# A graph network's edge stage on one core: SyncE fetches the set-aside rows one round earlier

## The chip, the cores and the metric

One core of a Trainium2 chip runs the whole program. The metric is device time in microseconds (us), the median of several executions. The engines are TensorE (PE, matmuls; PEld its weight loads), VectorE (DVE), ScalarE (ACT), GpSimd (POOL) and SyncE (SP, which here only issues transfers). A name with a q (SPq, ACTq) is that engine's instruction queue, where DMA issues stand.

## The reference, cut to what matters

Two graph layers over 6,250 nodes and 200,000 edges, sorted by destination. The stage that the change touches is the second layer, per edge:

```python
w = jax.nn.silu(rbf @ We1 + be1) @ We2 + be2      # edge_attr (200000 x 64) -> 128 per edge
m = w * (h[src] @ Wlin)                           # row of lin_table, picked by src
agg = jax.ops.segment_sum(m, dst, num_segments=h.shape[0])
out = jax.nn.silu(agg @ Wn1 + bn1) @ Wn2 + bn2
return h + out
```

## The kernel before

`h @ Wlin` stands in device memory as `lin_table` (one 512-byte row per node) when the edge stage begins. The edges are cut into G = 196 groups of 1,024 (8 tiles of 128 edges), and four groups make a round; there are ITERS = 49 rounds. Buffers are a ring of RING = 4 slots, so a round fills each slot once.

For every group, in this order:

- SP loads 1,024 rows of edge_attr into the slot of `ea` (`load_ea`, L505; one 256 KB transfer). It may do so when the group four back has been transposed (`ea_turned`).
- PE transposes them (`turn_ea`, L1678), ACT copies the result (`features`, L849), PE multiplies by We1 (`layer1`, L1686), ACT applies silu (`silus`, L856), PE multiplies by We2 (`layer2`, L1693 and L1697) into the PSUM tensor pb.
- POOL gathers the source rows tile by tile into the slot of `gat` (`gather`, L596, indirect DMA of 128 rows), by an index column that ACT copies (`next_idx`, L727) after its other work for a group.
- DVE multiplies pb by the rows (`messages`, L1336) and counts `msg_ready`, two per group. POOL may refill the slot after that.
- DVE compares destinations (L1340), PE sums by destination (`group_sums`, L1714), DVE adds the sums (L1353).

PE runs the groups as a software pipeline: for group g it does layer2(g), layer1(g+1), turn_ea(g+2), group_sums(g-1).

The eighth tile of the fourth group of a round is set aside: for rounds 1 to PICKS = 47 POOL does not gather it. Its 128 rows are fetched one by one with plain 512-byte transfers into `aside[par]` (two buffers, by the round's parity): 72 by SP and 56 by ACT, in four chunks of 18 and 14. `fetch_rows` does a chunk: a register load of the list (L418), then the transfers (L422). In the messages of that fourth group DVE waits for `sp_rows_in[par]` and `act_rows_in[par]`, then multiplies three quarters at L1330 and the last quarter with the aside rows at L1332. ACT fetches the rows of round it+1 while it handles round it (`source_rows`, with a wait on `msg_ready` at L860 before the first chunk). SP's `load_turn(it)` loads the four edge groups of round it, and after each of them fetches a chunk of round it-1.

Of the kernel before, what the change touches and what calls it, by code (L numbers as in the profile page):

```python
# [32 lines left out]
RING = 4  # L33
# [22 lines left out]
PICKS = ITERS - 2  # L56
SP_ROWS = 72
# [12 lines left out]
def gnn_kernel(nc, x, src, dst, edge_attr, W1, b1, W2, b2, We1, be1, We2, be2, Wlin, Wn1, bn1, Wn2, bn2, out):  # L70
    ctx = ExitStack()
    with ctx:
# [3 lines left out]
        def sem(name):  # L76
            return ctx.enter_context(nc.semaphore(name))
# [54 lines left out]
        def part(mem, at, n, dt=fp32):  # L132

            v = mem[:, at:at + n]
            return v if dt is fp32 else v.bitcast(dt)
# [77 lines left out]
        sp_list = part(table_w, 2 * F, PICKS * SP_ROWS, int32)[0:1, :].rearrange("a (k r) -> a k r", r=SP_ROWS)  # L213
# [154 lines left out]
        sp_rows_in = [sem(f"sp_rows_in{i}") for i in range(2)]  # L368
# [10 lines left out]
        msg_ready = sem("msg_ready")  # L379


        passed = sem("passed")
# [57 lines left out]
        def _(sp):  # L440
# [76 lines left out]
            def load_turn(it, par=None):  # L517
                for s in range(RING):
                    sp.wait_ge(ea_turned, it * RING + (s - RING + 1))
                    load_ea(it * RING + s, s)  # L520
                    if par is not None:
                        fetch_rows(sp, sp_list, it - 1, par, s, 0, SP_ROWS // RING, sp_rows_in)
            load_turn(1)
            with sp.Fori(0, PICKS // 2) as i:
                load_turn(i * 2 + 2, 1)
                load_turn(i * 2 + 3, 0)
            for s in range(RING):
                g = (ITERS - 1) * RING + s
                sp.wait_ge(ea_turned, g - RING + 1)
                fetch_rows(sp, sp_list, PICKS, 1, s, 0, SP_ROWS // RING, sp_rows_in)  # L530
                if g < G - 1:
                    load_ea(g, s)
                else:

                    rest = g * GE + FULL_TAIL * P
                    sp.dma_start(ea[:, s, 0:FULL_TAIL * RBF].rearrange("p (u f) -> p u f", u=FULL_TAIL),
                                 edge_attr[g * GE:rest, :].rearrange("(u p) f -> p u f", u=FULL_TAIL)).then_inc(ea_loaded[s], 16)
                    sp.dma_start(ea[0:N_EDGES - rest, s, FULL_TAIL * RBF:(FULL_TAIL + 1) * RBF],
                                 edge_attr[rest:N_EDGES, :]).then_inc(ea_loaded[s], 16)
# [1254 lines left out]
```

## Time and profile before

| | us |
|---|---|
| median of 3 executions (4439.01 to 4446.9) | 4445.35 |
| the profiled execution | 4483.88 |
| its span, first to last instruction | 4482.2 |
| stretch 0 to 1444: first layer, node work | 1444 |
| stretch 1444 to 1525: the edge stage begins, no row fetched by SP yet | 81 |
| stretch 1525 to 4423: SP fetches rows of rounds 1 to 47 | 2898 |
| stretch 4423 to 4482: last groups, output | 59 |
| TensorE's granted clock in the third stretch, share of full speed | 0.70 |
| busy in the third stretch: PE, POOL, DVE, ACT | 1594, 1393, 766, 387 |

Busy time counts an engine's own work; issuing transfers, register work and waiting are not busy. No engine is busy for even 60% of the third stretch, so what sets its length has to be looked for in the queues and waits.

### The profile page before, as it was taken

To read this page: it belongs to the slowest core of one execution; us is meant where nothing else is said; L and a number is where in the kernel's file an instruction comes from. 1 tells how busy PE (TensorE), PEld (TensorE's weight loads), DVE (VectorE), ACT (ScalarE), POOL (GpSimd) and SP (SyncE) were. 2 spreads that over 40 slices of the span, in tenths; PEclk is the share of its full clock that TensorE was granted. 3 is DMA by queue.
4 is the path that set the end of the run, shared out by engine and by line. 5 is a ranking of instruction groups with operands and counts; after the bars stand their busy time and mean duration, and the time that the engine had idled before them with its cause. 6 is when DMAs were issued, how large, how long until landed. Compare 5 with 4: busy or idle time off the path is not lost.

```text
span 4482.2 us, 78117 instructions
## 1 busy us (share of the span) xinstructions
PE 2954.2 (66%) x18158; PEld 2128.8 (47%) x18159; DVE 1957.4 (44%) x4445; ACT 963.7 (22%) x2058; POOL 1504.8 (34%) x1605
## 2 busy tenths in 40 slices
PE   4789999999799554565555555545655555555547
PEld 2335667676599333443333443334433334433335
DVE  4999998888744322222222222222222222222223
ACT  3213345555311211111111111111111111111111
POOL 5000000000000544544454544444444445444442
PEclk6999999999899676766666766666777676777668
DMA  2001122222397211211121212111211121111212
GB/s 63 1 30 58 73 87 100 104 102 102 158 354 284 59 53 51 53 51 50 49 54 51 55 49 53 51 52 52 53 48 51 52 53 53 50 52 51 53 50 57
DMA packets 291040, 327.33 MB, mean 73 GB/s; under 512 B 237087, under 2 KB 250424, under 8 KB 278174
## 3 DMA queue, kind: packets, MB, share of 16 engines
q1 hardware_dynamic: 234382, 218.90, 14.7%
q0 software_dynamic: 51072, 104.27, 8.1%
q14 instruction: 302, 2.47, 0.2%
q10 hardware_dynamic: 5264, 1.36, 0.1%
q8 instruction: 20, 0.33, 0.0%
HBM read 239.30 MB, written 85.09 MB: 72 GB/s over the span
## 4 chain that ended last, share of the span: by engine, by line
SPq 42%; issue 29%; PE 13%; DVE 10%; DVEq 4%; another core or an unknown queue 2%; DMA 0%; ACT 0%; POOL 0%; ACTq 0%; POOLq 0%
SPq L422 28%; SPq L418 10%; DVE shared L1131 3%; SPq L505 3%; PE pc L1522 3%; PE pd L1522 3%; PE pb L1528 2%; PE pa L1528 2%; DVE c L1131 1%; DVE c L1136 1%; DVEq L1131 1%; DVE hch L1131 1%; DVE loop L1131 1%; PE pb L1613 1%
## 5 line engine op out<-in xcount | busy, mean ns | idle before, releaser
L596 POOL DMA_INDIRECT shared<-lin_table,idx x1516 | 1434.0, 946 | 1531.4 <-ACT idx L727 616.2
L1336 DVE TENSOR_TENSOR shared<-pb,shared 128x512 f32<-128x512 f32 x345 | 233.1, 688 | 1608.8 <-DMA table_sb<-lin_table 1297.0
L1697 PE MATMUL pb<-we_sb,shared 128*128 128x128 f32 x3136 | 679.0, 382 | 346.9 <-ACT shared L856 334.1
L1693 PE MATMUL pb<-be_parts,ones 3*128 3x512 bf16 x392 | 189.3, 483 | 952.4 <-DVE shared L1336 933.2
L1697 PEld LDWEIGHTS pb<-we_sb,shared 128*128 128x128 f32 x3136 | 577.4, 275 | 484.4 <-ACT shared L856 367.2
L1693 PEld LDWEIGHTS pb<-be_parts,ones 3*128 3x128 bf16 x392 | 36.9, 94 | 1014.8 <-issue 988.4
L625 POOL DMA_DIRECT2D lin_table<-c x12 | 9.1, 760 | 1347.8 <-ACT c L802 1347.8
L1131 DVE TENSOR_SCALAR shared<-col_h,shared 128x784 bf16<-128x784 f16 x1092 | 407.4, 424 | 11.0 <-issue 10.7
L727 ACT ACTIVATE idx<-idx_all 128x8 int32 (+1 forms) x196 | 40.6, 209 | 1647.1 <-issue 1647.1
L856 ACT ACTIVATE shared<-pa,be_col 128x512 f32<-128x512 f32 x392 | 257.3, 685 | 627.4 <-PE pa L1686 344.8
L1686 PE MATMUL pa<-shared,we_sb 64*128 64x512 f32 x784 | 312.9, 887 | 7.9 <-issue 7.0
L1528 PE MATMUL pb<-shared,c 128*128 128x392 bf16 x1568 | 306.0, 330 | 5.2 <-DVE shared L1131 0.9
L1522 PE MATMUL pc<-table_sb,shared 128*128 128x192 bf16 x2450 | 237.1, 248 | 30.6 <-DVE table_sb L1082 30.0
L1353 DVE TENSOR_TENSOR agg<-agg,pf 128x128 f32 x98 | 28.3, 289 | 520.5 <-remote 413.9
L1522 PEld LDWEIGHTS pc<-table_sb,shared 128*128 128x128 bf16 x2450 | 226.2, 142 | 45.2 <-issue 31.0
L1340 DVE TENSOR_TENSOR shared<-pe_iota,dl_f 128x1024 f32<-128x1024 f32 x196 | 240.0, 1225 | 6.7
L1340 DVE TENSOR_TENSOR shared<-pe_iota,dst_f 128x1024 f32<-128x1024 f32 x196 | 238.1, 1215 | 0.0
L758 ACT ACTIVATE shared<-pa 128x784 bf16<-128x784 f32 x196 | 161.2, 822 | 315.7 <-PE pa L1528 315.7
L1522 PE MATMUL pd<-table_sb,shared 128*128 128x192 bf16 x2352 | 225.4, 246 | 0.0
L1522 PEld LDWEIGHTS pd<-table_sb,shared 128*128 128x128 bf16 x2352 | 215.7, 142 | 12.8
L758 ACT ACTIVATE shared<-pb 128x784 bf16<-128x784 f32 x196 | 161.6, 824 | 280.2 <-PE pb L1528 280.2
L1714 PE MATMUL pf<-shared 128*128 128x128 f32 x1568 | 211.6, 292 | 14.3 <-issue 12.4
(273 smaller groups left out, 3699.2 us busy)
## 6 DMA issues: line engine op xcount, KB each, us to landing
adjacency<-shared SPq DMA_DIRECT2D x49, 1568.0 KB, 5.6
shared<-adjacency SPq DMA_DIRECT2D x49, 1568.0 KB, 8.7
table_sb<-lin_table SPq DMA_DIRECT2D x3384, 0.5 KB
shared<-in_edge_attr_dram SPq DMA_DIRECT2D x195, 256.0 KB
table_sb<-lin_table ACTq DMA_DIRECT2D x2632, 0.5 KB
shared<-lin_table,idx POOLq DMA_INDIRECT x1516
lin_table<-c POOLq DMA_DIRECT2D x12, 256.0 KB, 7.4
out_dram<-xr SPq DMA_DIRECT2D x12, 256.0 KB
```

Of the source, the lines that this page charges most:

```text
L418: eng.load(regs, table[:, bass.ds(k - 1, 1), chunk * here:(chunk + 1) * here].rearrange("a k r -> a (k r)"))
L422: eng.dma_start(aside[par][row:row + 1, :].bitcast(uint8), lin_bytes[:, bass.ds(at, ROW_BYTES)]).then_inc(rows_in[par], 16)
L596: pool.indirect_dma_start(out=dest(s, j), out_offset=None, in_=table, in_offset=bass.IndirectOffsetOnAxis(ap=idx[:, s, j:j + 1], axis=0)). ...
L758: act.activation(adj[i][:, w * WC:(w + 1) * WC].rearrange("p (h c) -> p h c", h=2), win_ps[w % 2][:, :, 0:WC // 2], ACT.Copy, accum_out=co ...
L856: act.activation(act_t[:, h, :], pa[:, h, :], ACT.Silu, bias=be1_col[:, :]).then_inc(hid_act, 1)
L1131: return dve.tensor_scalar(to, col_h[:, :], keys[i][:, ahead:KC][:, bass.ds(tile, 1)], float(-WC * w), ALU.subtract, ALU.is_equal)
L1336: dve.tensor_tensor(msgs[s % 2][:, h, :, :], pb[:, h, :].rearrange("p (i f) -> p i f", f=F), rows[:, h, :, :], ALU.mult).then_inc(msg_read ...
L1340: return dve.tensor_tensor(to[:, :, :], iota_ps.rearrange("p (a d) -> p a d", a=1).to_broadcast([P, U, P]), bc(offsets, P), ALU.is_equal)
L1522: last = pe.matmul(bank[:, 0:TW], by_source[:, h, :], table_sb[:, h, :], start=(h == 0), stop=(h == NB - 1))
L1528: last = pe.matmul(ps[:, h, 0:WC // 2], lo, col[:, h * WC // 2:(h + 1) * WC // 2], start=first, stop=end)
L1686: pe.matmul(pa[:, h, :], we1_sb[half, :], ea_t[half, :], start=True, stop=True).then_inc(hid_mm, 1)
L1697: last = pe.matmul(pb[:, h, i * F:(i + 1) * F], act_t[:, h, i * P:(i + 1) * P], we2_sb[:, :], start=False, stop=(i == 3))
```

## The change

SP fetches a chunk of round it, not of round it-1, in `load_turn(it)`. So turn 1 now has fetches, the turn after the loop has none, and the parities swap. Since the buffer `aside[par]` may then still be read for round it-2, SP waits before the first chunk for the messages through round it-2 (`msg_ready` of 8 per round), as ACT does.

```diff
                     sp.wait_ge(ea_turned, it * RING + (s - RING + 1))
                     load_ea(it * RING + s, s)
                     if par is not None:
-                        fetch_rows(sp, sp_list, it - 1, par, s, 0, SP_ROWS // RING, sp_rows_in)
-            load_turn(1)
+                        if s == 0 and not isinstance(it, int):
+                            sp.wait_ge(msg_ready, (it - 1) * (2 * RING))
+                            sp.sem_inc(passed, 1)
+                        fetch_rows(sp, sp_list, it, par, s, 0, SP_ROWS // RING, sp_rows_in)
+            load_turn(1, 1)
             with sp.Fori(0, PICKS // 2) as i:
-                load_turn(i * 2 + 2, 1)
-                load_turn(i * 2 + 3, 0)
+                load_turn(i * 2 + 2, 0)
+                load_turn(i * 2 + 3, 1)
             for s in range(RING):
                 g = (ITERS - 1) * RING + s
                 sp.wait_ge(ea_turned, g - RING + 1)
-                fetch_rows(sp, sp_list, PICKS, 1, s, 0, SP_ROWS // RING, sp_rows_in)
                 if g < G - 1:
                     load_ea(g, s)
```

The order of SP's instructions moves at three places; nothing moves on another engine. Lines behind the edit are two or three higher in the changed program. First, SP where the edge stage begins, turn 1 and the head of the loop:

```order
-L505 DMA shared<-in_edge_attr_dram 128x8x64 x4
-L524 UNCONDITIONAL_BRANCH
-L524 ISA
+L505 DMA shared<-in_edge_attr_dram 128x8x64
+L418 TENSOR_LOAD table_sb
+L422 DMA table_sb<-lin_table 1x512 x18
+L505 DMA shared<-in_edge_attr_dram 128x8x64
+L418 TENSOR_LOAD table_sb
+L422 DMA table_sb<-lin_table 1x512 x18
```

The four edge loads of turn 1 stood together; each now has a list load and 18 row fetches behind it. Second, SP at the head of a turn inside the loop, with the semaphores that are waited for:

```order
 L505 ISA [waits ea_turned]
 L505 DMA shared<-in_edge_attr_dram 128x8x64
-L418 ISA
+L523 ISA
+L418 ISA [waits msg_ready]
 L418 TENSOR_LOAD table_sb
 L422 DMA table_sb<-lin_table 1x512 x18
```

One register instruction is added and the wait stands between the turn's first edge load and its list load. Third, SP behind the loop, before (the loop's own branch is the second row):

```order
-L524 REGISTER_ALU
-L524 COMPARE_AND_BRANCH
-L418 TENSOR_LOAD table_sb
-L422 DMA table_sb<-lin_table 1x512 x18
-L505 DMA shared<-in_edge_attr_dram 128x8x64
-L418 TENSOR_LOAD table_sb
-L422 DMA table_sb<-lin_table 1x512 x18
-L505 DMA shared<-in_edge_attr_dram 128x8x64
```

and in the changed program:

```order
+L527 REGISTER_ALU
+L527 COMPARE_AND_BRANCH
+L505 DMA shared<-in_edge_attr_dram 128x8x64 x3
+L538 DMA shared<-in_edge_attr_dram 128x2x64
+L540 DMA shared<-in_edge_attr_dram 64x64
```

The last round's edge loads stood between fetches of round 47; they now follow each other when all fetches are issued.

## Rows read from the trace of the kernel before

**Rows 1.** The page: span, and the chain that ended last by line.
```profile
span 4482.2 us, 78117 instructions
...
SPq L422 28%; SPq L418 10%; DVE shared L1131 3%; SPq L505 3%; PE pc L1522 3%; PE pd L1522 3%; PE pb L1528 2%; PE pa L1528 2%; DVE c L1131 1%; DVE c L1136 1%; DVEq L1131 1%; DVE hch L1131 1%; DVE loop L1131 1%; PE pb L1613 1%
```
**Rows 2.** Waits, 1900 to 4400: who waited for whom, total us, times, longest.
```profile
DVE shared L1336 <- DMA table_sb<-lin_table: 1140.7, 41, 34.5
...
PE pb L1693 <- DVE shared L1336: 819.6, 40, 28.4
```
**Rows 3.** Waits of SP's own queue, 1900 to 4400 (the only row).
```profile
SPq L418 <- PE pd L1678: 3.2, 1, 3.2
```
**Rows 4.** Timeline of SP, one turn: start, us, instructions merged by line.
```profile
3017.88 0.40 SPq L505 DMA_DIRECT2D shared<-in_edge_attr_dram  x1
3020.11 11.24 SPq L422 DMA_DIRECT2D table_sb<-lin_table  x18
3031.62 0.40 SPq L505 DMA_DIRECT2D shared<-in_edge_attr_dram  x1
3036.10 6.96 SPq L422 DMA_DIRECT2D table_sb<-lin_table  x18
3045.96 0.01 SPq L505 DMA_DIRECT2D shared<-in_edge_attr_dram  x1
3048.79 10.26 SPq L422 DMA_DIRECT2D table_sb<-lin_table  x18
3060.47 0.69 SPq L505 DMA_DIRECT2D shared<-in_edge_attr_dram  x1
3064.44 13.73 SPq L422 DMA_DIRECT2D table_sb<-lin_table  x18
3078.47 0.40 SPq L505 DMA_DIRECT2D shared<-in_edge_attr_dram  x1
```
**Rows 5.** Timeline of POOL, same turn: a burst's first and last gather, the next's first.
```profile
3021.10 0.95 POOL L596 DMA_INDIRECT shared<-lin_table,idx  x1 [9.60 <-DVE shared L1332]
...
3028.61 0.95 POOL L596 DMA_INDIRECT shared<-lin_table,idx  x1 [0.30 <-issue]
3038.74 0.95 POOL L596 DMA_INDIRECT shared<-lin_table,idx  x1 [9.18 <-ACT idx L727]
```
**Rows 6.** Timeline of SP in its last turn: two chunks of 18 fetches.
```profile
4380.99 21.77 SPq L422 DMA_DIRECT2D table_sb<-lin_table  x18
...
4416.86 5.74 SPq L422 DMA_DIRECT2D table_sb<-lin_table  x18
```
**Rows 7.** POOL's gathers (L596) by stretch: us, busy and count, PE clock, DMA.
```profile
3018.90:3079.90 61.00, 29.34 (x31) 0.70 0.20 53
1474.80:1523.20 48.40, 30.81 (x33) 0.61 0.26 68
...
4380.00:4403.00 23.00, 15.14 (x16) 0.73 0.16 47
4416.00:4423.00 7.00, 0.00 (x0) 0.64 0.04 11
```
**Rows 8.** Timeline of SP where the edge stage begins.
```profile
1474.77 48.82 SPq L505 DMA_DIRECT2D shared<-in_edge_attr_dram  x5
1525.47 22.17 SPq L422 DMA_DIRECT2D table_sb<-lin_table  x18
```
**Rows 9.** Timeline of ACT: two index copies, idle time since the copy L849.
```profile
3037.65 0.21 ACT L727 ACTIVATE idx<-idx_all 128x8 int32 x1 [5.81 <-issue]
...
3050.68 0.21 ACT L727 ACTIVATE idx<-idx_all 128x8 int32 x1 [11.10 <-issue]
```
**Rows 10.** Timeline of PE behind the last fetch: one group's layer2 to the next's.
```profile
4424.62 0.58 PE L1693 MATMUL pb<-be_parts,ones 3*128 3x512 bf16 x1 [10.93 <-DVE shared L1336]
...
4434.06 0.39 PE L1693 MATMUL pb<-be_parts,ones 3*128 3x512 bf16 x1
```
**Rows 11.** The page, DMA issues: KB each, us from issue to landing.
```profile
shared<-adjacency SPq DMA_DIRECT2D x49, 1568.0 KB, 8.7
```

## The prediction

> **What bounds the kernel now.** I read the chain that ended last first: SP's queue, a list load and row fetches, is its largest named part [rows 1], and all of that lies behind 1525. The waits say who is held up: DVE stands 1,141 us in 41 waits, 27.8 us each, for a row transfer, and PE then stands behind DVE [rows 2]. From this alone the rows look late, and fetching them a round earlier looks like the cure.
>
> So I asked next why they are late, in SP's own waits: in 2,500 us its queue waits 3.2 us for anything [rows 3]. SP is never idle. Its timeline shows a turn from edge load to edge load, 3017.88 to 3078.47, so 60.6 us, filled end to end: four blocks of 18 fetches, 42.2 us, and four headers (edge load, list load) of 18.4 us together [rows 4]. The rows are late because SP issues them at the rate at which it can, and takes up the next turn at once. What bounds the stage is SP's throughput, 47 turns of it.
>
> What sets SP's rate is the second reading. With no gather on POOL 18 fetches took 5.74 us, 0.32 us each; a block that ran beside 16 gathers took 21.77 us, 1.21 us each [rows 6, 7]. That is 16 us for 16 gathers: a gather beside fetches costs SP about 1.0 us, though it lasts 1.25 us (3021.10 to 3028.61 is six steps) [rows 5]. A turn has 31 gathers [rows 7]: 72 fetches at 0.32 are 23 us, the gathers add some 19, the headers 18; that is the 60.6.
>
> **The change part by part.** The sum is made against the profiled execution, 4483.9 us (span 4482.2 and 1.7 around it). The median of the three runs is 38.5 us below it, and I take that off at the end.
>
> *Fetches per turn*: none removed, none added. SP still issues 72 fetches, four edge loads and four list loads a turn, beside 31 gathers. Being a round ahead lets DVE go sooner, and DVE, PE and ACT then run ahead until the next thing that SP delivers is missing, which is the edge load: PE transposes group n when it has landed, and SP issues load n+1 one block of fetches later. The stall moves from DVE's row wait to PE's transposition; cost 0.
>
> *Where the gathers fall within a turn*: this can change. Now two headers of a turn run free of gathers (2.5 and 4.75 us) and two beside them (5.7 and 5.4) [rows 4, 5], so a header, mean 5.6 instead of 3.6, loses 0.35 us per us of gather, and fetches lose 1.0/1.25 = 0.8. Each us of gather that moves from fetches to headers saves SP 0.45 us. Now 11.1 of 31 x 1.25 = 38.8 us lie on headers. The bounds: all four headers covered (22.4 us) is -5.1 us a turn, none is +5.0. After the change all groups are alike, paced by their edge load. It must land and be transposed, which has no row of its own: more than nothing, and less than the 8.7 us in which a load of six times its bytes landed [rows 11]; I take 4 with ACT's copy, nearer to the small end since a sixth of the bytes is moved. 5.8 to 11.1 us after its copy ACT has fetched its 14 rows and copies the index [rows 9], and the gather starts 1.1 us later (3037.65 to 3038.74) [rows 5, 9]. So it runs from 11 to 16 us after an edge load until 21 to 26 us, which in a block of 15.2 us is until 6 to 11 us after the next edge load. A header lies from 1 us ahead of its edge load to 4.5 us behind it: wholly inside in the early case, two thirds inside in the late one. I take 12 us of headers covered, less than either, because ACT's fetches slow down beside a gather as well and push the next one back. That is 0.5 us less a turn, times 46: -23 us. Bounds -235 and +230.
>
> *The start*: SP passes the list's wait at 1474.77 but its first fetch stands at 1525.47, behind edge loads that wait for transposes until 1523.6 [rows 8]. The fetch can now follow the first of these loads as closely as it did the fifth: 48.4 us earlier. This is the one sure gain, and it is once, not per turn. Against it, 33 gathers of 1474.8 to 1523.2 [rows 7] now meet fetches. At the other end, behind the last fetch, I count two more groups of gathers outstanding than now (16). Net 17 gathers at 1.0 us: +17 us, between 0 and +33.
>
> *The new wait*: behind it stand SP's list load, 18 fetches and the next edge load; DVE waits for the former, PE for the latter. It asks for messages of a round whose rows were all issued one full turn (60 us) ago. It should never hold. The register instruction costs under 0.1 us where SP runs freely and up to some 0.7 beside gathers (half of 1.21, as a fetch is two instructions): 5 to 32 us over 46 turns; I take 5, since the list load behind it has slack.
>
> *The end*: the last edge loads used to be issued among the fetches. They now follow the last one, so the last messages with fetched rows wait for a load, a transpose, sums and a layer2. One group took 9.4 us from layer2 to layer2 just after the last fetch [rows 10], of which none was waiting for loads: +10 us, between 5 and 25.
>
> Sum: -23 -48 +17 +5 +10 = -39, so 4445 us in a profiled execution and **4406 us** as a median.
>
> A rule of the Trainium skill speaks for much more: DMA: Bandwidth & Descriptors, "Issuing engines are not separate DMA queues", says that the sequencer's time to initiate a DMA is usually small relative to the DMA, and its "Rules for kernel authors" say to issue early and wait late, so that the fixed cost overlaps. By that rule all of the 1,141 us could be hidden. This trace disagrees on the size: at 0.32 to 1.21 us per fetch, 72 a turn, issue is what fills SP.
>
> **The rivals.** *A, likeliest:* SP stays the bound, a turn changes by under 1 us; 4406, between 4360 and 4450. Chance 0.55. That the change does next to nothing is the upper edge of this case.
>
> *B: headers slip wholly under the gathers.* For it: every header will then be in the same place relative to a gather, and the early case above covers it. With 3 us less a turn: -138 -16 = 4290. Chance 0.18.
>
> *C: slower, gathers fall on fetches alone.* If ACT's fetches end so late that a gather starts some 20 us after its edge load, headers run free and fetches take the load. With 2.5 us more a turn: +115 -16 = 4545. Against it: a slower SP lengthens the block, which moves the gather forward in it again. It decides from about 0.35 us a turn, where the 16 us of the other terms are used up. Chance 0.20.
>
> *D: the wait was mere lateness*, as the rule has it. Then the stall goes and a turn falls to what POOL needs, 38.8 us and some idle time between bursts, say 45: -16 x 46 = -736, about 3700. It would need SP to issue 72 fetches beside 31 gathers in 45 us, which took 60 throughout. Chance 0.04.
>
> *E: the new wait holds SP*, as DVE's messages run late. A hold of 10 us a turn would be +460, about 4870. It needs messages more than four groups behind SP, and SP's ring wait, which stands at the same distance, held for 3.2 us in all [rows 3]. Chance 0.03.
>
> **How the numbers follow.** The prediction is A's. The range takes A and B whole and C up to its middle: 4285 to 4515, which leaves out D, E and the far parts of B and C. Within 0.2% (9 us) is what a measurement here can tell from no change. A has 0.40 faster, 0.12 same, 0.03 slower; B and D are faster, C and E slower: 0.62, 0.12, 0.26.
>
> **What would show it.** DVE's wait for rows falls from 1,141 us to under 100, and its place is taken by PE waiting at the transposition and DVE behind PE, about as much in total. SP's queue still runs without waits, a turn from edge load to edge load at 60 to 61 us. SP's first fetch stands near 1477 and the last some 50 us earlier than now, with about 70 us behind it instead of 60. The prediction is wrong if SP shows waits at its list load (E), if a turn is under 58 or over 63 us (B, C), or if its turns have idle time (D): then issue was not the bound.

## The result: 4194 us, 5.7% faster

The changed kernel took 4194.45 us (median of three, 4180.4 to 4195.41) where the kernel before took 4445.35 us: a ratio of 0.943, with a 95% interval of 0.940 to 0.946. In a later session the change came to 4182.36 us and the kernel before to 4448.66 (0.940, 0.937 to 0.943). Over all sessions the kernel before lay between 4445 and 4489 us, the change at 4182 and 4194; so an experiment is judged by its own median and by its turn in the trace, with the ratio beside it. In the sessions of e1 to e8 the kernel before took 4488 and 4489 us and the change was not run, so a difference of under 1% between one of those runs and 4194 us is not told apart. For two of them (e12, e14) disturbed executions move the median, and there the ratio, which leaves those out, is used.

The forecast was 4406 us, 4285 to 4515. The sign was right; the size was not: 39 us less were forecast and 251 measured.

### The profile page after: what moved, and what is told of

The parts are those of the page before. It is cut to its first block, busy times and chain, and to the rows that moved or that the text cites. A ratio compares the mean times of both kernels' runs of the same rounds, so it can differ in the third digit from the quotient of the medians.

```text
span 4178.8 us, 78209 instructions
## 1 busy us (share of the span) xinstructions
PE 3017.7 (72%) x18158; PEld 2225.0 (53%) x18159; DVE 1955.4 (47%) x4445; ACT 962.4 (23%) x2058; POOL 1499.1 (36%) x1605
## 4 chain that ended last, share of the span: by engine, by line
SPq 43%; issue 27%; PE 16%; DVE 9%; DVEq 3%; DMA 0%; ACT 0%; another core or an unknown queue 0%; POOL 0%; ACTq 0%; POOLq 0%
SPq L422 29%; SPq L418 12%; PE pc L1524 4%; PE pb L1530 3%; PE pa L1530 3%; DVE shared L1133 3%; PE pd L1524 3%; SPq L505 2%; DVE c L1133 1%; DVEq L1133 1%; DVE c L1138 1%; DVE hch L1133 1%; DVE loop L1133 1%; PE pb L1615 1%; DVEq L1171 0%
## 5 line engine op out<-in xcount | busy, mean ns | idle before, releaser
L1680 PE MATMUL pd<-ident,shared 128*128 128x128 f32 x784 | 202.4, 407 | 871.3 <-DMA shared<-in_edge_attr_dram 871.1
L1680 PEld LDWEIGHTS pd<-ident,shared 128*128 128x128 f32 x784 | 129.2, 202 | 1037.5 <-DMA shared<-in_edge_attr_dram 1024.8
L1699 PE MATMUL pb<-we_sb,shared 128*128 128x128 f32 x3136 | 489.2, 301 | 27.7 <-issue 20.0
L1699 PEld LDWEIGHTS pb<-we_sb,shared 128*128 128x128 f32 x3136 | 412.3, 205 | 138.0 <-issue 129.4
L1133 DVE TENSOR_SCALAR shared<-col_h,shared 128x784 bf16<-128x784 f16 x1092 | 404.5, 419 | 11.3 <-issue 11.1
L1355 DVE TENSOR_TENSOR agg<-agg,pc 128x128 f32 x98 | 28.3, 288 | 800.9 <-remote 630.4
L1716 PE MATMUL pc<-shared 128*128 128x128 f32 x1568 | 341.3, 405 | 50.4 <-issue 50.4
L1716 PEld LDWEIGHTS pc<-shared 128*128 128x128 f32 x1568 | 319.7, 311 | 80.5 <-issue 80.4
L1716 PE MATMUL pf<-shared 128*128 128x128 f32 x1568 | 343.2, 408 | 19.7 <-issue 17.8
L1716 PEld LDWEIGHTS pf<-shared 128*128 128x128 f32 x1568 | 321.9, 313 | 55.0 <-issue 52.9
L851 ACT ACTIVATE shared<-pd 128x512 f32<-128x512 f32 x196 | 117.0, 597 | 583.6 <-issue 362.2
```

The costliest lines, as they stand in the source:

```text
L1133: return dve.tensor_scalar(to, col_h[:, :], keys[i][:, ahead:KC][:, bass.ds(tile, 1)], float(-WC * w), ALU.subtract, ALU.is_equal)
L1680: last = pe.transpose(pd[:, i * P:(i + 1) * P], ea[:, s, i * P:(i + 1) * P], ident[:, :])
L1699: last = pe.matmul(pb[:, h, i * F:(i + 1) * F], act_t[:, h, i * P:(i + 1) * P], we2_sb[:, :], start=False, stop=(i == 3))
L1716: last = pe.matmul(lin_sums[s % 2], msgs[s % 2][:, h, i, :], hot_f[s % 2][:, 2 * i + h, :], start=(h == 0 and i == 0), stop=(h == 1 and i ...
```

## The profile after

The page of the changed kernel: the span and the chain that ended last, by engine and by line.

```profile
span 4178.8 us, 78209 instructions
...
SPq 43%; issue 27%; PE 16%; DVE 9%; DVEq 3%; DMA 0%; ACT 0%; another core or an unknown queue 0%; POOL 0%; ACTq 0%; POOLq 0%
SPq L422 29%; SPq L418 12%; PE pc L1524 4%; PE pb L1530 3%; PE pa L1530 3%; DVE shared L1133 3%; PE pd L1524 3%; SPq L505 2%; DVE c L1133 1%; DVEq L1133 1%; DVE c L1138 1%; DVE hch L1133 1%; DVE loop L1133 1%; PE pb L1615 1%; DVEq L1171 0%
```

By this chain alone nothing has changed: row fetches and list loads on SP's queue lead it as in [rows 1]. The waits from 1900 to 4100 (who waited for whom, total us, times, longest) show what has:

```profile
DVE agg L1355 <- remote: 1133.2, 114, 12.5
...
PE pd L1680 <- DMA shared<-in_edge_attr_dram: 763.1, 160, 7.7
```

DVE's wait for rows [rows 2] has no row any more. In its place PE waits at nearly every transposition for an edge load, 4.8 us on average and 763 us in all, three quarters of the 1003 us that DVE waited for rows in the same window before. SP's own waits, the view of [rows 3], came back empty for these 2,200 us: the queue still never waits, at the new list wait neither. Yet a turn, from edge load to edge load in SP's timeline, is shorter:

```profile
3005.45 0.39 SPq L505 DMA_DIRECT2D shared<-in_edge_attr_dram  x1
3007.83 10.49 SPq L422 DMA_DIRECT2D table_sb<-lin_table  x18
3018.59 0.40 SPq L505 DMA_DIRECT2D shared<-in_edge_attr_dram  x1
3023.08 10.21 SPq L422 DMA_DIRECT2D table_sb<-lin_table  x18
3033.55 0.40 SPq L505 DMA_DIRECT2D shared<-in_edge_attr_dram  x1
3035.76 9.74 SPq L422 DMA_DIRECT2D table_sb<-lin_table  x18
3045.71 0.40 SPq L505 DMA_DIRECT2D shared<-in_edge_attr_dram  x1
3050.20 10.26 SPq L422 DMA_DIRECT2D table_sb<-lin_table  x18
3060.75 0.40 SPq L505 DMA_DIRECT2D shared<-in_edge_attr_dram  x1
```

This turn takes 55.3 us, 40.7 in blocks and 14.6 in headers; the one in [rows 4] took 60.6, of it 42.2 and 18.4. The larger part of the difference is in the headers, which hold the same instructions but for one register instruction and the new wait. What differs beside them is where the gathers lie. POOL's timeline, same turn, the first gather of each burst (in brackets its idle time before and what ended it):

```profile
3004.87 0.94 POOL L598 DMA_INDIRECT shared<-lin_table,idx  x1 [4.05 <-DVE shared L1338]
...
3018.68 0.94 POOL L598 DMA_INDIRECT shared<-lin_table,idx  x1 [4.14 <-ACT idx L729]
...
3033.11 0.94 POOL L598 DMA_INDIRECT shared<-lin_table,idx  x1 [4.76 <-DVE shared L1338]
...
3046.33 0.94 POOL L598 DMA_INDIRECT shared<-lin_table,idx  x1 [4.79 <-DVE shared L1338]
...
3060.16 0.94 POOL L598 DMA_INDIRECT shared<-lin_table,idx  x1 [4.16 <-DVE shared L1338]
```

Every burst starts within 0.6 us of an edge load on SP, 4.0 to 4.8 us after the one before. In [rows 5] the idle time before a burst was 9.60 and 9.18 us; the two bursts after those came 3.32 and 0.90 us behind the one before. Of the bursts with idle time before them, from 1900 to 4000, the middle four fifths start between 0.7 us ahead of the nearest edge load and 1.3 us behind it, after 3.9 to 5.1 us of idle time; in the kernel before between 5.8 us ahead and 6.8 us behind, after 1.0 to 10.5 us. The order in time for the second burst of this turn can be followed on PE and ACT: the edge load issued at 3005.45 has landed and is transposed at 3008.98, ACT copies it, issues its 14 fetches, copies the index, and the next burst begins at 3018.68, with the next edge load.

```profile
3008.98 1.12 PE L1680 MATMUL pd<-ident,shared 128*128 128x128 f32 x4 [6.84 <-DMA shared<-in_edge_attr_dram]
```

```profile
3010.22 0.60 ACT L851 ACTIVATE shared<-pd 128x512 f32<-128x512 f32 x1 [5.01 <-issue]
3011.80 5.63 ACTq L422 DMA_DIRECT2D table_sb<-lin_table  x14
3017.58 0.21 ACT L729 ACTIVATE idx<-idx_all 128x8 int32 x1 [6.77 <-issue]
```

ACT's index copy is one of two things that release a burst; the other, more often the last to come, is DVE's messages of the group four back. POOL's waits from 1900 to 4100:

```profile
POOL shared L598 <- DVE shared L1338: 409.9, 90, 5.8
...
POOL shared L598 <- ACT idx L729: 278.1, 67, 4.5
```

TensorE's granted clock rose too, from 0.69 to 0.75 of full speed (1900 to 4000). It does not order the kernels: e17, below, has a shorter turn than the change at 0.72, and PE stands waiting for edge loads in the change.

The two ends of the edge stage, in SP's timeline: its first edge load and block, the last block of the first round, and the last block of all with the edge loads behind it.

```profile
1476.30 0.39 SPq L505 DMA_DIRECT2D shared<-in_edge_attr_dram  x1
1478.49 34.66 SPq L422 DMA_DIRECT2D table_sb<-lin_table  x18
...
1555.62 11.12 SPq L422 DMA_DIRECT2D table_sb<-lin_table  x18
...
4100.73 7.44 SPq L422 DMA_DIRECT2D table_sb<-lin_table  x18
4108.23 2.20 SPq L505 DMA_DIRECT2D shared<-in_edge_attr_dram  x3
```

The spans differ by 303.4 us (4482.2 to 4178.8; the profiled execution of before was 38 us above its median, this one 14 below). Its parts: the 72nd fetch starts at 1566.7 instead of 1601.3, -34.6; from there to the last fetch (4107.5 instead of 4422.4) 46 turns take 55.23 us instead of 61.33, -280; behind the last fetch stand 71.3 us instead of 59.8, +11.5. The medians differ by 251 us and not by 303; with the same two ends that leaves about 5.0 us a turn instead of 6.1 (an estimate from these numbers). A second trace of the change (e16) has a turn of 55.4 us.

**The whole edge stage on one line per kernel.** From SP's timeline, over 46 turns: a block is the time from the start of its first fetch to that of its last, a header the rest up to the next first fetch. The last column is the part of the gathers (38.7 us a turn) that lies on headers once the first turns are over; it is good to about half a microsecond, and e3 has 1.8 over all 46 turns.

```
                        median  ratio   turn  headers blocks  gathers on headers
before                  4445    1       61.3   19.8    41.5   10.0
change                  4194    0.943   55.2   15.8    39.5   12.3
e1 bursts late          4248    0.947   56.3   15.7    40.6   12.0
e2 memsets, idle time   4289    0.956   57.1   15.7    41.4    9.5
e3 change, 64/64        4176    0.930   55.2   11.6    43.5    0.9
e4 before, 64/64        4149    0.925   54.2   13.2    41.0    9.5
e5 80-byte lists        4203    0.936   55.6   11.3    44.3    4.9
e6 list load first      4324    0.964   58.0   16.3    41.8    5.1
e7 change, 16 rows      4303    0.959   57.8   15.8    42.0   15.1
e8 before, 16 rows      4571    1.019   63.3   15.6    47.7    5.6
e9 one chunk later      4211    0.946   56.0   17.0    38.9   13.9
e10 two chunks later    4393    0.988   59.9   19.4    40.6   11.9
e13 ACT in one transfer 4373    0.982   59.2   16.8    42.3    8.3
e15 index first, padded 4324    0.972   58.9   15.3    43.6   10.9
```

Four blocks of 18 would take 4 x 17 x 0.32 = 21.8 us free of gathers. What is above that, over the gathers that do not lie on headers, is the price of a gather on fetches: before 19.7/28.7 = 0.69 us per us, change 17.7/26.4 = 0.67; for the other rows with 72 fetches and full gathers it lies between 0.60 and 0.71 (e15: 0.78), with 64 fetches (19.2 us free) at 0.64 and 0.75, with gathers of 16 rows at 0.86 and 0.78. So from before to the change the price hardly moved. What differs is how much of the gathers lies on fetches, and how long the headers are. This is an account of where SP's time went; it does not show by itself what set the turn.

## The experiments

**e1, e2: are the bursts' starts what counts? Four memsets on POOL, between its waits and the gathers (e1) or ahead of the waits (e2).**

```diff
                 for s in range(RING):
+                    (e2: the memsets here)
                     pool.wait_ge(lin.idx_ready, it * RING + (s + 1))
                     pool.wait_ge(msg_ready, (it * RING + (s - RING + 1)) * 2)
                     pool.sem_inc(passed, 1)
+                    for n in range(4):          # e1
+                        pool.memset(c1[:, 0:CB, :], 0.0).then_inc(raw_set, 1)
+                        pool.wait_ge(raw_set, (it * RING + (s - RING)) * 4 + (n + 4))
+                        pool.sem_inc(passed, 1)
                     gather(lin, lin_table, linear_rows, s, tiles if s == RING - 1 else U)
```

> The change kept, with four GpSimd memsets of an idle buffer (some 3.5 us) between GpSimd's waits and each chunk's gathers, so that each burst starts some 3.5 us after SyncE's edge load instead of with it. Theory (a burst's onset costs nothing because it lies on SyncE's edge load and list load; a microsecond of gather that lies on row fetches slows them): the bursts slide onto the fetches, a turn grows from 55.3 us to 58 to 63 us, the kernel by 130 to 360 us over the change's 4194, to about 4325 to 4555. Rival 1 (a fixed lag: whatever SyncE does, the slowing begins some 4.7 us after the first gather because the edge load's own transfer comes first): the slow part slides too but keeps its length, turn 55.3 within 0.5 us, 4170 to 4220. Rival 2 (the gain is the earliness of the rows, not the place of the gathers): the same as rival 1, and DVE's wait for a row stays gone.

> Control for the one before: the same four memsets, but ahead of GpSimd's waits, where GpSimd idles 4 to 5 us between bursts, so that they work as much and move the bursts little. Theory: within 30 us of the change's 4194. If memsets by themselves slow VectorE or SyncE: slower by the same amount as the kernel with the late bursts.

Measured 4248 and 4289 us. Both expectations of the theory were missed, e1 lies above its rivals' 4170 to 4220 as well, and the control was the slower of the two. POOL's timeline of e1 says why: its bursts still start with SP's edge loads (3000.57, 3014.55), and POOL has no idle time left.

```profile
3000.46 0.95 POOL L598 DMA_INDIRECT shared<-lin_table,idx  x1 [0.81 <-POOL c L643]
...
3010.17 0.87 POOL L643 MEMSET c<- 128x896 f32 x1
...
3014.84 0.95 POOL L598 DMA_INDIRECT shared<-lin_table,idx  x1 [0.81 <-POOL c L643]
```

The memsets filled the 4 us in which POOL had waited. A burst every 14.4 us by POOL's own work is 57.5 us for four of 8 gathers, 56.2 with the 31 of a turn: the turn of 56.3. In e2 a burst comes every 14.6 us in the same way, which makes 57.1, again its turn; its bursts start 1.0 us behind an edge load (median). So these two hardly moved the bursts; they made POOL the bound. They also give a warning: SP's queue shows no waits here either, though POOL sets the pace. SP stretches to what the gathers leave it, so that a queue without waits does not prove that it is the bound.

**e3, e4: 64 rows of a round on SP and 64 on ACT instead of 72 and 56**, in the change (e3) and in the kernel before (e4).

```diff
-SP_ROWS = 72
+SP_ROWS = 64
```

> The change kept, with SyncE fetching 64 rows of a round instead of 72 and ScalarE 64 instead of 56. Theory (after the change SyncE's issuing still sets the turn, 4 headers and 72 fetches): 8 fetches fewer at 0.33 us (free of gathers) to 0.55 us (the mean) are 2.6 to 4.4 us a turn less, 120 to 205 us in all, 3990 to 4075. Rival (with the rows early, SyncE's count no longer sets the turn; PE, the edge loads or ScalarE do): 4194 within 20 us, or slower where ScalarE's longer list holds it up.

> The kernel before, with the same split of 64 and 64. Theory (SyncE's issuing sets the turn before the change too): 2.6 to 4.6 us a turn less, 120 to 210 us under the kernel before. If it comes out under the change's 4194, the same time was to be had without the change. Rival (before the change it is the lateness of the rows, a round of 128 fetches whoever makes them, that sets the turn): within 20 us of the kernel before.

Measured 4176 and 4149 us. In the change, 8 fetches fewer on SP gained little: the theory's 120 us are missing, and the rival is right about the time (by the ratios, 0.930 and 0.943, it may be 1%). In the kernel before the same edit gained 339 us within its session, far more than the 120 to 210 expected, and beats the change. The table says where: of the 7.2 us a turn the headers give 6.6 and the blocks 0.5. The list loads of 16 numbers take 0.85 us in e4 (mean, 1900 to 4100) where those of 18 took 2.06, which is 4.8 us a turn. So it is hardly the 8 fetches that pay there. SP's timeline of e3 shows where the fetches' gain went:

```profile
3022.12 0.40 SPq L505 DMA_DIRECT2D shared<-in_edge_attr_dram  x1
3023.91 11.07 SPq L422 DMA_DIRECT2D table_sb<-lin_table  x16
3035.29 0.40 SPq L505 DMA_DIRECT2D shared<-in_edge_attr_dram  x1
```

16 fetches take 11.1 us where 18 took 10.2, and edge load to first fetch is 1.8 us where it was 2.4 and 4.5. The list loads had become shorter, and the bursts, behind two more fetches on ACT, start 2.4 us after an edge load: nearly all on fetches. The list load itself was the next suspect.

**e5: each list of 18 row numbers starts on a multiple of 80 bytes. e6: the list load ahead of the edge load.**

```diff
-sp_list = part(table_w, 2 * F, PICKS * SP_ROWS, int32) ... r=SP_ROWS
+sp_list = part(table_w, 2 * F, PICKS * RING * SP_STEP, int32) ... c=RING, r=SP_STEP      # e5, SP_STEP = 20
```
```diff
 regs = [...]
 eng.load(regs, table[...])
+load_ea(it * RING + s, s)          # e6, moved here from ahead of the list load
 for n in range(here):
```

> The change kept, but each chunk's list of 18 row numbers starts on a multiple of 80 bytes in SBUF, not 72. Second theory, formed from the first four runs: SyncE is never idle in either kernel, and its turn is the list loads and edge loads (the headers), 0.32 us for each fetch, and some 0.6 us more for each microsecond of gather that lies on fetches; gathers on a list load cost nothing. In the changed kernel the list loads take 1.56 and 3.85 us by turns, in the kernels with 16 numbers a list 1.13, so the start of the list at 72 bytes is the suspect. If so, all take 1.2 to 1.6 us, the headers come to 10 to 11 us a turn from 15.8, more of the gathers falls on fetches, and a turn is 52.1 to 54.5 us: 35 to 145 us under 4194, 4050 to 4160. Rival 1: the list's start does not matter, list loads stay at 1.56 and 3.85, 4194 within 15. Rival 2: list loads get shorter, but something other than SyncE holds a turn at 55 us, 4180 to 4210.

> The change kept, with each chunk's list load ahead of its edge load instead of behind it. The gathers start with the edge load, so that the list load now lies in the gap between two bursts. Second theory (what made the turn shorter is that the gathers lie on the list loads, where they cost nothing): the gathers under the headers fall from 12.3 us a turn to 1 or 2, the fetches lose 6 to 7 us more. If the list loads stay as long as they are (1.56 and 3.85), a turn is 61 to 62 us, 265 to 310 over 4194, about 4460 to 4505, so that the whole gain is gone; if they shrink to about 1 us because no edge load stands ahead of them, it is 55 to 56.5 us, 4180 to 4250, and the trace must show both. Rival 1 (only the earliness of the rows counts): 4194 within 20 with list loads as long as before. Rival 2 (a list load ends at a fixed time after the edge load's issue): list loads of 1 us or less.

The list loads on SP, one row for each kernel (duration in ns, min/median/max), first the change, then e5, then e6:

```profile
L418 SPq TENSOR_LOAD <-table_sb x160: 1555/1661/3874, 1908.6 to 4098.9; - x160
```
```profile
L423 SPq TENSOR_LOAD <-table_sb x160: 1555/1560/1582, 1899.8 to 4093.9; - x160
```
```profile
L418 SPq TENSOR_LOAD <-table_sb x153: 1555/1574/3860, 1902.6 to 4098.1; - x153
```

In e5 the long list loads are gone, the headers are 4.5 us a turn shorter, and the turn is not (55.6): the gathers came off the headers, from 12.3 to 4.9 us, and the blocks grew by 4.8 us. In time the second rival was right. In e6 the list loads are as long as in the change, now free of gathers where they were mostly covered, so a gather on one costs nothing; now they lie between bursts, and the turn grows by 2.8 us, 4324 us. The direction is the theory's, the size is under half of its 6 to 7. Both fit that a microsecond of gather that goes from a list load to a fetch costs SP, and e5 that the gain of a shorter header is lost by it. But e3 and e5 keep the turn of the change with 38 and 34 us of gathers on fetches, where the change has 26, so the place of the gathers alone does not set that turn; e17 comes back to this.

In the kernel before the list loads are not always so long. Behind an edge load that was held up many are shorter, some next to nothing, so that the mean list load takes 2.06 us before and 2.69 in the change:

```profile
L418 SPq TENSOR_LOAD <-table_sb x143: 4/1568/3871, 1911.1 to 4090.0; - x143
```

**e7, e8: gathers of 16 rows instead of 128**, in the change and in the kernel before (112 rows of each tile are not fetched).

```diff
-out=dest(s, j), ... ap=idx[:, s, j:j + 1]
+out=dest(s, j)[0:n], ... ap=idx[0:n, s, j:j + 1]      # n = 16 in the edge stage
```

> The change kept, but each edge-stage gather fetches 16 rows instead of 128 (the other rows of the gathered tiles are left as they are, so the messages are not the reference's). To be read against the kernel before with the same edit. Second theory (the difference of the two kernels is what the gathers cost SyncE, by where they fall): with an eighth of the bytes the loss all but goes, a turn is 38 to 45 us, 3370 to 3700, and the two kernels end within 0.5 us a turn (25 us) of each other but for some 30 us at the start and 10 at the end. Rival 1 (earliness of the rows): the changed kernel stays some 250 us the faster. Rival 2 (it is the number of gather instructions that counts, not their bytes): both stay where they are, 4194 and 4445.

> The kernel before, with gathers of 16 rows instead of 128 (the messages are not the reference's). Second theory: 3400 to 3730, and 0 to 45 us over the changed kernel with the same gathers. Rival 1 (earliness): some 250 us over it. Rival 2 (number of gathers, not bytes): 4445 within 30.

Measured 4303 and 4571 us. e8 is 82 us over the kernel before of its session, e7 109 over 4194; the difference between the two is kept. What GpSimd's queue moved from 1900 to 4000, first the change, then e7:

```profile
q0 software_dynamic: 37871, 77.65, 14.3%
```
```profile
q0 software_dynamic: 36416, 9.40, 1.9%
```

An eighth of the bytes at the same number of packets slows SP no less. The gathers' count disturbs the fetches, or that of their packets, which is as large as before, and not their data, as the second rival said; why the turn even grew (57.8 and 63.3 us) stays open. That the difference survives does not speak for earliness, though the first rival expected it: in e8 just 5.6 us of gather lay on headers, in e7 15.1.

**e9, e10: SP's fetches one chunk and two chunks later than in the change.** In the change DVE takes a round's rows 13.1 us (median of 47) after SP's last fetch of them; before, 1.6 us after it.

```diff
 load_ea(it * RING + s, s)
+if s < 2:                                   # e10; 1 in e9
+    fetch_rows(sp, sp_list, it - 1, 1 - par, s + RING - 2, ...)
+    continue
 ...
-fetch_rows(sp, sp_list, it, par, s, ...)
+fetch_rows(sp, sp_list, it, par, s - 2, ...)
```

> The change kept, but SyncE fetches each quarter of a round's rows one chunk later than in the change (the last quarter in the first chunk of the next round). In the changed kernel VectorE takes the rows 13.1 us (median) after SyncE's last fetch of the round, in the kernel before 1.6 us after it, that is as soon as they land. One chunk is 13.8 us, so the margin is used up to within a microsecond. Theory (VectorE's wait for the rows, once a turn, stops every other engine and bunches the gathers behind it; without it each chunk's edge load paces the gathers, which then begin with SyncE's list load, where they cost nothing): at the edge, a turn of 55 to 58 us, 4180 to 4320. Rival (the gain is in the order of SyncE's queue or in the earlier start, not in that wait): 4194 within 25.

> As the one before, two chunks later. The margin is 14 us short. Theory: VectorE waits for the rows again in every round, the gaps between bursts spread from 4 us to a range of 1 to 10 or more, and a turn is 59 to 62 us, 4370 to 4500, most of the gain gone although SyncE issues the same fetches behind the same edge loads as in the change. Rival: 4194 within 25 us.

Measured 4211 and 4393 us, turns of 56.0 and 59.9: both as the theory expected. e9 lies within its rival's 25 us too, so that e10 decides. With one chunk DVE waits 3.0 us a round for rows (117.6 us in 39 waits); with two it waits as in [rows 2], the bursts are unevenly spaced again, and the headers are back at 19.4 us. DVE's wait, and the bursts of one turn of e10 on POOL:

```profile
DVE shared L1343 <- DMA table_sb<-lin_table: 980.9, 40, 27.5
```
```profile
3022.63 0.95 POOL L603 DMA_INDIRECT shared<-lin_table,idx  x1 [11.59 <-ACT idx L734]
...
3036.33 0.94 POOL L603 DMA_INDIRECT shared<-lin_table,idx  x1 [5.24 <-DVE shared L1343]
...
3049.70 0.95 POOL L603 DMA_INDIRECT shared<-lin_table,idx  x1 [3.66 <-ACT idx L734]
```

4.7 of the 6.1 us a turn are lost again, with the same fetches behind the same edge loads. The start is hardly delayed (the 72nd fetch stands at 1569.9 us, in the change at 1566.7), so the gain per turn hangs on that wait; one chunk of margin is all it needs. SP's queue waits 0.7 us in all from 1900 to 4000 in e10, so SP does the same work in 59.9 us a turn as in 55.2 in the change: with DVE's wait the time changes that SP's instructions take.

**e11, e12, e17: what is left when SP fetches no single rows.** e11 has no row fetches at all, a 32nd gather brings the rows; in e12 and e17 SP brings its 18 rows of a chunk as one transfer of neighbours (not the rows that are wanted). e16 is the change itself.

```diff
-gather_turn(it, ASIDE)
+gather_turn(it, U)                          # e11, fetch_rows gone on SP and ACT
```
```diff
+if table is sp_list:                        # e12, e17; act_list in e13
+    eng.dma_start(aside[par][row:row + here, :], lin_table[0:here, :]).then_inc(rows_in[par], 16)
+    return
```

> No row fetches at all: the 128 rows of a round that SyncE and ScalarE fetch one by one are gathered by GpSimd with a 32nd gather, as in the first round. SyncE keeps the edge loads alone. Theory (SyncE's queue, which is never idle in either kernel, sets the turn of both): PE no longer waits for edge loads, and a turn falls to the next bound, GpSimd's 32 gathers at 1.25 us, 40 us, and what lies between bursts: 40 to 51 us, 3490 to 4000. Rival (a turn of 55 us is a floor that another loop sets, since the changed kernel and two of its variants all came to 55.2 to 55.6): 4194 to 4260, with bursts 4 us apart as before.

> The change kept, but SyncE fetches its 18 rows of a chunk in one transfer of 18 neighbouring rows, not the rows that are wanted (so the messages are not the reference's); its list loads and all of ScalarE's single fetches stay. If SyncE's issuing sets the changed kernel's turn of 55.2 us: a turn falls to about 50 to 52 us (51.8 was measured with no fetches and one gather more), 3950 to 4050. If ScalarE's 14 fetches ahead of its index copy set it: 54 to 55.5 us, 4140 to 4200. If the two together (they compete for one path): about half way, 52 to 54.

> The change itself once more, as the measure for the other runs, since the kernel before came out between 4445 and 4489 us in different runs. If the change shifts as the kernel before does, its ratio stays 0.940 to 0.946; if only the kernel before does, its own median stays at 4180 to 4200.

> SyncE's 18 fetches of a chunk as one transfer once more (messages not the reference's), beside the change itself, to read what holds the turn when SyncE is free: 4090 to 4130 us, 1 to 2.3 us a turn under the change; SyncE's queue waits for transposes, and GpSimd's bursts wait for ScalarE's index copy, which stands behind its 14 fetches. If SyncE's issuing alone set the turn of the change, 3950 to 4050.

e11 took 4041 us (ratio 0.907, 0.906 to 0.909), the fastest kernel here. A turn from edge load to edge load is 51.7 us, just outside the 40 to 51 expected, as the time is outside 3490 to 4000; SP now waits most of the time (1900 to 3950):

```profile
SPq L505 <- remote: 1552.5, 97, 27.9
SPq L505 <- PE pd L1675: 237.1, 43, 9.8
```

e12 came to 0.924 and e17 to 0.934 of the kernel before; beside the change (4182 us, e16) e17 took 4145 us, 15 us over its range, and its turn is 54.0 us against 54.9 measured the same way. e16 fits both of its cases. SP's queue of e17 stands free (1900 to 4000, as the next two rows):

```profile
SPq L511 <- remote: 853.2, 78, 22.1
SPq L511 <- PE pd L1686: 657.5, 70, 16.0
SPq L530 <- DVE shared L1340: 150.2, 15, 18.7
```
```profile
POOL shared L604 <- ACT idx L735: 480.6, 76, 12.4
...
PE pb L1705 <- ACT shared L864: 390.0, 90, 13.7
```

So 72 fetches fewer on SP are worth about 1 us a turn in the change; by e12's ratio it would be nearer 2 (an estimate). By these waits it is then ACT that holds the turn, with 14 fetches ahead of its index copy and its next activations; no run takes ACT's fetches away from e17, but without any fetches and with a gather more (e11) the turn is 51.7 us. That the change had come to within one or two microseconds of its next bound is also the likeliest reason why e3 and e5 gained so little.

**e13: ACT's 14 rows as one transfer of neighbours. e14: the index copy ahead of ACT's fetches. e15: e14 with the lists of e5.**

```diff
+after_gather(lin, it, s, 1 if s == RING - 1 else 0)      # e14, e15: moved up
 source_rows(it + 1, par, s)
-after_gather(lin, it, s, 1 if s == RING - 1 else 0)
```

> The mirror image: ScalarE fetches its 14 rows of a chunk in one transfer of neighbouring rows (messages not the reference's), SyncE its 18 one by one. If ScalarE's fetches, which stand between the edge load's landing and the index copy that releases the next burst, set the turn: 50 to 52 us, 3950 to 4050. If SyncE sets it: its fetches lose the competition with ScalarE's (0.97 us beside gathers and ScalarE, 0.63 beside gathers alone), 52 to 54 us, 4040 to 4130. If neither: 55.

> The change kept, with ScalarE's index copy (which releases a burst of gathers) ahead of its 14 row fetches instead of behind them. Nothing is left out. If the chain edge load, transposition, ScalarE's copy, 14 fetches, index copy, burst sets the turn: bursts start up to 5 us earlier after an edge load, the idle time between bursts falls from 4 us towards 3, a turn 51 to 53.5 us, 4000 to 4115. If SyncE's own queue sets it: the bursts move by as much, over the ends of SyncE's fetches and its edge load, and a turn stays at 54.5 to 56.5 us, 4160 to 4250. If VectorE's release (it ends half of the waits) comes at the same time: nothing moves, 4194 within 20.

> The one before with list starts on multiples of 80 bytes as well. In the changed kernel the shorter list loads gained nothing, because the gathers then started a microsecond later against the headers. If that is why (bursts come a fixed time after an edge load, so a shorter turn puts them later in it), bursts that can come earlier give the gain back: 2 to 4 us a turn under the kernel with the index copy first alone. If another loop holds the turn: the same as that kernel within 0.5 us a turn, 25 us in all.

All three were slower than the change, against every expectation: 4373 us (0.982), 0.979 (0.974 to 0.984) and 4324 us (0.972). Without ACT's fetches in the chain, a burst does not start with the next edge load but 5 us after one, in the middle of a block, or just ahead of one. SP and POOL in e13:

```profile
3009.44 0.40 SPq L511 DMA_DIRECT2D shared<-in_edge_attr_dram  x1
3013.92 9.89 SPq L428 DMA_DIRECT2D table_sb<-lin_table  x18
3025.23 0.00 SPq L511 DMA_DIRECT2D shared<-in_edge_attr_dram  x1
3026.98 5.90 SPq L428 DMA_DIRECT2D table_sb<-lin_table  x18
```
```profile
3015.25 0.94 POOL L604 DMA_INDIRECT shared<-lin_table,idx  x1 [10.20 <-ACT idx L735]
...
3030.42 0.95 POOL L604 DMA_INDIRECT shared<-lin_table,idx  x1 [6.72 <-ACT idx L735]
```

e13 takes 56 competing fetches away, DVE takes the rows 23 us after SP's last fetch, and still a turn is 59.2 us: 1.0 more in headers and 2.8 more in blocks than in the change. SP's queue shows no wait. So rows that come early do not bring the change's turn by themselves. The bursts are spaced unevenly in e13, as before the change (10.20, 6.72 and 4.62 us of idle time in this turn, and then two bursts without any between them). That this is what costs fits the rows; no run moves the bursts and nothing else. e15 against e14 (intervals 0.970 to 0.975 and 0.974 to 0.984) is too close to say whether the shorter lists gain there.

## Why the prediction failed, step by step

**What bounds the kernel before**: neither proven nor refuted. e4 gained 339 us with less work on SP, most of it from shorter list loads. But SP's work is no fixed amount of time: e10 does it in 59.9 us a turn and the change in 55.2, and its queue shows no wait where POOL sets the pace (e1). The reading that counts for this was [rows 3]: a queue without waits was taken for the bound. The kernel before without SP's fetches, the counterpart of e17, was not run.

**Fetches per turn, and where the stall goes**: right about the place of the stall. DVE's row wait vanished, PE now waits for edge loads (763 us) and DVE behind it, and SP's queue shows no wait.

**The start, the new wait, the end**: right. First fetch at 1478.5 (near 1477 was forecast), -34.6 us where -48 + 17 = -31 stood; no wait at the list; +11.5 where +10 stood.

**Where the gathers fall within a turn**: this is the step that failed. It was priced at -0.5 us a turn (0.9 us of gather at 0.45 are nearer 0.4) and measured -6.1 between the profiled executions, about -5.0 by the medians: ten times as much, at its own bound of -5.1 or past it. A turn under 58 us was named as a sign of being wrong, and it came. The forecast that a gather starts 11 to 16 us after an edge load holds (13.2 us in the turn above). That 12 us of gather on headers were taken and 12.3 measured is partly luck: the 12 was set below both cases worked out, of 22.4 us of headers, and the headers of the change have 15.8. The price was wrong. It took 0.35 us of header per us of gather, a mean over two headers that were wholly covered [rows 4, 5]. There, gathers lay on the last fetch, the edge load and the list load alike. In the trace these take them differently. From the end of the last fetch to the edge load SP spent 0.37 us in the 71 headers of the kernel before that were free of gathers and 2.14 in the 33 that were wholly covered (1900 to 4100); from the edge load to the end of the list load 3.27 and 3.08; from there to the first fetch 0.10 and 0.59. So a wholly covered header does cost 2.1 us more, near the 2.0 of the prediction, but edge load and list load together take nothing of it. In the change, where bursts start with the edge load, the three parts are 0.32, 3.28 and 0.10 us (mean of 160), as in a header free of gathers, although most of it is covered; before, the means of all were 1.34, 3.10 and 0.30 (144). Times four, that is about the -4.0 us of headers a turn; the blocks give -2.0, from 2.3 us of gather that came off the fetches and from their price (0.69 to 0.67, where 0.8 was taken).

The term thus missed two things: that the removed wait would space the bursts evenly, and that a header covered from its edge load on costs SP no more than a free one.

**The rivals.** B had the direction, headers under the gathers, and with -3 us half the size. C did not come; e6 and e13 show that other places of the gathers go with a slower turn, if not one slower than before. D, mere lateness, was given 0.04 as a fall to 45 us. The runs show both sides of it. e10 shows, with e9, that the margin of the rows carries the gain, so the wait was the lever. That it works through the place of the gathers is argued from the rows; e13, slow with no row late, fits it. The rival reading, that the turn fell to its next bound and SP's instructions merely filled what was left, is not excluded: e3 and e5 keep the turn with the gathers elsewhere. The next bound, which D put at 45 us, was at about 54 (e17). The rule named in the prediction (the Trainium skill, DMA: Bandwidth & Descriptors, "Rules for kernel authors": issue early and wait late) pointed the right way here; the margin that paid was one chunk, 13.1 us. The other sentence named there, that the time to initiate a DMA is usually small relative to the DMA itself (the Trainium skill, DMA: Bandwidth & Descriptors, "Issuing engines are not separate DMA queues"), is not borne out for these 512-byte fetches: they take 0.32 to 1.21 us of SP each [rows 6], where DVE takes a round's rows 1.6 us after the last of them.

**What stays open.** Whether SP or ACT ends last in a turn of the change: by e17 and e12 they are within 1 or 2 us, and SP's fetches beside gathers take 1.14 us while ACT fetches too and 0.53 while it does not (means in the change, 1900 to 4100). The sums with 0.67 are an account of measured places, not a forecast of them. In the turn shown, the chain edge load, ACT's fetches, index copy, burst is about as long as a quarter of a turn (13.2 and 13.8 us); that the even spacing comes from this is not shown, nor for which other lengths it would hold.

## What to carry to other kernels

A queue that never waits is not yet the bound: if its instructions slow down beside another engine's work, it fills whatever time there is, and one must take its work away (e17) to see what it was worth. When a wait that stops everything once a round is removed, ask where the other engines' bursts will then start against this queue's instructions, and price each kind of instruction there by itself, since a mean over a mixed stretch hid that some were free. And compare with the plain way: one more gather in place of 128 single fetches (e11) beat all the orders of those fetches.

## What the runs showed of the hardware that was not expected

- A load of 18 row numbers into registers takes 1.56 and 3.85 us by turns in the change, where lists start every 72 bytes, and 1.56 at each where they start every 80 (e5); 16 numbers every 64 bytes took a median of 1.14 us (e3). That the start's alignment does it is the nearest reading; a multiple of 80 was the only other step tried with 18.

```profile
L418 SPq TENSOR_LOAD <-table_sb x159: 700/1142/1156, 1905.1 to 4082.7; - x159
```

- Gathers slow single fetches by their number, or that of their packets, and not by their bytes (e7: 9.4 MB instead of 77.65 at a like number of packets, and a turn 2.6 us longer).
- Taking a competitor away can cost: with ACT's 56 fetches as four transfers the kernel was 4% slower (e13); that the gathers then started at a worse place is the nearest reading.
